# VectorE's program written out for all steps in a one-core attention and mixture-of-experts layer

## The reference

```
x = x + attention(layernorm(x))     # 16 heads, keys of 16, values of 64, no softmax: relu(q.k)^2
x = x + moe(layernorm(x))           # 16 experts of width 64, 4 chosen per token, plus a shared expert
```

## Time and profile before

| | us |
|---|---|
| median of three runs | 830.85 |
| lowest, highest | 829.86, 833.11 |
| the profiled execution, its own time | 831.47 |
| its span, first to last instruction | 829.5 |

### The profile page before, as it was taken

How to read it: one execution, slowest core, us unless ns; L and a number is a source line. 1 busy time by engine, 2 the same in 40 slices (tenths; PEclk the granted TensorE clock), 3 DMA queues, 4 the chain that set the end, 5 groups by cost and what they waited for, 6 DMA issues and landing times.

```text
span 829.5 us, 16902 instructions
## 1 busy us (share of the span) xinstructions
PE 691.8 (83%) x5160; PEld 545.1 (66%) x5160; DVE 520.7 (63%) x1739; ACT 434.9 (52%) x986; POOL 352.7 (43%) x368
## 2 busy tenths in 40 slices
PE   1576897979979797988979797997979799797785
PEld 1444476858767685867758585876758587676675
DVE  3545667576666748576575757667475856666654
ACT  2466674565646464564646456464655556453211
POOL 2246563644435353544535264453526444363100
PEclk9878998999989898998989899898989999898898
DMA  8994849091835619092562909174371908300000
GB/s 194 132 144 48 131 87 108 14 144 24 124 48 95 72 60 113 6 139 32 94 72 73 98 18 137 24 113 58 79 87 36 128 1 126 40 15 1 8 7 7
DMA packets 72814, 60.94 MB, mean 73 GB/s; under 512 B 8624, under 2 KB 72496, under 8 KB 72752
## 3 DMA queue, kind: packets, MB, share of 16 engines
q1 hardware_dynamic: 72752, 60.26, 49.4%
HBM read 41.37 MB, written 18.87 MB: 73 GB/s over the span
## 4 chain that ended last, share of the span: by engine, by line
PE 57%; DVE 25%; issue 9%; ACT 4%; DMA 2%; DVEq 1%; POOL 1%; SPq 1%; ACTq 0%; POOLq 0%
PE ps_a L503 11%; PE ps_f L365 8%; PE ps_f L428 7%; PE ps_f L367 6%; PE ps_f L366 6%; PE ps_f L447 5%; PE ps_s L474 5%; PE ps_f L424 4%; DVE norms_m L741 2%; PE ps_f L407 2%; DMA qkt<-qk_rows 2%; DVE it L852 2%; PE ps_f L418 2%; DVE norms_t L661 2%; DVE norms_t L662 2%
## 5 line engine op out<-in xcount | busy, mean ns | idle before, releaser
L334 POOL TENSOR_TENSOR p<-r 128x512 f32<-128x512 f32 x256 | 262.5, 1046 | 392.4 <-ACT r L603 392.4
L603 ACT ACTIVATE r<-ps_s 128x512 f32<-128x512 f32 x256 | 138.5, 596 | 81.0 <-PE ps_s L474 79.8
L503 PE MATMUL ps_a<-p,v 128*64 128x256 f32 x1024 | 143.5, 396 | 3.4 <-DVE big L897 2.2
L897 DVE TENSOR_TENSOR big<-ps_a,wt 128x256 f32<-128x256 f32 x128 | 53.7, 420 | 73.7 <-ACT big L612 51.1
L503 PEld LDWEIGHTS ps_a<-p,v 128*64 128x64 f32 x1024 | 64.4, 138 | 41.7 <-POOL p L334 2.7
L852 DVE TENSOR_TENSOR it<-ps_f,it 128x256 f32<-128x256 f32 x144 | 59.1, 420 | 44.0 <-ACT it L595 41.0
L595 ACT ACTIVATE it<-ps_f 128x256 f32<-128x256 f32 x144 | 55.2, 383 | 50.1 <-PE ps_f L367 47.7
L418 PE MATMUL ps_f<-ident,cs 128*32 128x128 f32 x32 | 9.2, 387 | 83.8 <-DVE cs L787 83.8
L447 PE MATMUL ps_f<-wdown,it 128*128 128x128 f32 x576 | 71.2, 279 | 2.9 <-DVE it L869 1.7
L869 DVE TENSOR_TENSOR it<-ps_f,it 128x512 f32<-128x512 f32 x64 | 44.0, 690 | 44.8 <-PE ps_f L424 44.3
L447 PEld LDWEIGHTS ps_f<-wdown,it 128*128 128x128 f32 x576 | 68.4, 195 | 4.5 <-DVE it L869 1.8
(11 more groups left out here) (153 smaller groups left out, 1607.2 us busy)
## 6 DMA issues: line engine op xcount, KB each, us to landing
qk_rows<-qk_parts SPq DMA_DIRECT2D x16, 1024.0 KB, 4.4
qkt<-qk_rows SPq DMA_DIRECT2D x64, 256.0 KB, 9.5
qkt<-qk_rows SPq DMA_DIRECT2D x128, 128.0 KB, 8.9
x_in<-in_L_attn_tokens SPq DMA_DIRECT2D x16, 128.0 KB, 2.2
x_res<-in_L_attn_tokens SPq DMA_DIRECT2D x16, 128.0 KB, 14.4
out<-o_sb SPq DMA_DIRECT2D x16, 128.0 KB, 14.2
big<-in_L_attn_Wqg SPq DMA_DIRECT2D x1, 640.0 KB, 4.2
big<-in_L_attn_Wkv SPq DMA_DIRECT2D x1, 640.0 KB, 5.3
```

The source lines that it names most:

```text
L334: pool.tensor_tensor(p[h % 4][:], r[h % 2][:], r[h % 2][:], ALU.mult).then_inc(probs_done, 1)
L503: last = pe.matmul(ps_a[k % 2][64 * e:64 * e + 64, 0:N], v[q][:, t, h * DV:(h + 1) * DV], p[h % 4][:, t * N:(t + 1) * N], start=(t == 0), ...
L603: act.activation(r[h % 2][:], ps_s[h % 2][:], ACT.Relu).then_inc(relu_done, 1)
L897: dve.tensor_tensor(aw[ap][:, pair, :], ps_a[pair % 2][:, 0:N], wt[ap][:, pair, :], ALU.mult)\
```

## The change

A second walker, `run_flat`, writes all 20 steps out, and VectorE uses it in place of `run_steps`. The steps of VectorE hold the same instructions on the same data in the same order. Every wait gets a constant, and the register instructions and the branch of the loop are gone from VectorE's program. For steps 4 to 13 the program text now has ten copies of a step where it had two. Nothing changes for the other four engines; TensorE, ScalarE and GpSimd keep the loop with register values.

```
+        def run_flat(step):
+
+            for s in range(FIRST_STEP, LAST_STEP + 1):
                 step(s, s % 2, stages(s), s)
...
-            run_steps(dve, step)
+            run_flat(step)
```

More of the change, by code:

```diff
@@ L200, in run_steps @@
             for s in range(LOOP_TO, LAST_STEP + 1):
+                step(s, s % 2, stages(s), s)
+        def run_flat(step):
+            for s in range(FIRST_STEP, LAST_STEP + 1):
                 step(s, s % 2, stages(s), s)
```

## The result

| | before | after |
|---|---|---|
| median, us (lowest, highest) | 831.24 (829.86, 833.11) | 820.25 (819.13, 821.27) |
| the profiled execution | 831.47 | 821.27 |
| its span | 829.5 | 819.5 |
| ratio to before, 95% interval | | 0.9863 [0.9847, 0.9879] |

The change makes the kernel faster by 1.4%, 11.0 us by the medians and 10.2 us between the two profiled executions. Lines behind the added function stand five further down: 787, 418 and 836 are now 792, 423 and 841.

What follows compares the result with a forecast made beforehand. The chain through TensorE and VectorE's small instructions ahead of `cs` was taken to bound the kernel. Jumps 4.1, registers 2.9 and 0.2 sum to 7.2 us, raised to 8.0 for the clock: 830.85 to 822.9, range 817 to 829.5.

Steps and rivals of the forecast that it cites:

- (3): TensorE's clock behind each restart: faster steps fall out of step with its rises; total gain taken as 8.0 us, not 7.2.
- What bounds the kernel: Chain through TensorE, VectorE's small dependent instructions and back with `cs`; VectorE's losses ahead of line 787 move TensorE's restart.
- fixed parts: Interval between TensorE restarts less 0.42 times the low-clock time: 44.99 written out, 45.28 in the loop, 46.30 with a jump.
- (1): VectorE's four jumps back go: each stalls 4.3 us, 1.02 us of it reaching the restart; 4.1 us, bounds 0 to 17.3.
- (2): VectorE's register work in steps 4 to 13 goes: 0.29 us a step, 2.9 us, plus 0.2 for the interval into step 4.
- Sum at an unchanged clock: Savings from VectorE's jumps and register work, with the low clock unchanged: 4.1 + 2.9 + 0.2 = 7.2 us.
- low stretches: Time TensorE runs at 1.2 GHz behind each restart, 2.71 to 5.78 us; each microsecond loses 0.42 us.
- the walk's first case: Stepping restarts against clock rises 47.8 us apart: one rise comes 3.4 us sooner in the 5.9 us step; 9.4 us gained.
- the second case: The early clock rise comes one step after the 5.9 us stretch; average stays 4.4 us and the gain is 7.2.
- Rival (a): Steps stay in step with clock rises if the fixed part exceeds 45.36 us, eating the gain: 829 to 833 us; chance 0.14.
- (c): TensorE, ScalarE or GpSimd needs its own reload at its loop's jump, returning 4.1 us: 827.0 us; chance 0.05.
- (d): VectorE's longer written-out program stalls while loading, 4.3 us a time: slower, 835 us or more; chance 0.05.

Runs made afterwards that it cites:

- the hint: The kernel before with its loop kept on VectorE and a branch hint at the head of each round: 828.13 us, ratio 0.9963.
- The pair of runs with 15 matmuls: 15 overwritten 128x512 matmuls per step ahead of TensorE's wait for `cs`: kernel before 801.98 us, changed kernel 793.04 us.
- the changed kernel with 36 matmuls: Changed kernel plus 36 overwritten 128x256 matmuls per step ahead of TensorE's wait for `cs`: 858.19 us, one of four executions 802.48.
- The stand-in at slot 0: Changed kernel plus 16 small dependent VectorE instructions at the head of slot 0 in steps 6, 8, 10 and 12: 835.35 us, ratio 1.0067.

## Why the prediction was right, and where it was off

Forecast 822.9 in 817.0 to 829.5; measured 820.25. The direction and the mechanism were right; the gain was 11.0 us where I had 8.0, and the shape of the steps came out right for a reason that is in part luck (see (3)).

- **What bounds the kernel: right.** The restarts behind the wait for `cs` move with everything VectorE loses ahead of line 787 and with the clock. Intervals without the low clock fall to the fixed parts within 0.2 us.
- **(1) The jumps: right in kind and in size.** Without jumps but with registers the fixed part is 45.26 where it was 46.30 and 45.28. Instructions to be loaded were the cause, since the hint removes the stall. The Trainium skill (Runtime: NRT & Kernel Launch, Instruction fetch mechanics) says that an engine loads its program ahead in sequence, so that a long program need not fit, and that a taken jump to a part no longer held must wait for it. The trace agrees: the longest wait of the kind "issue" in VectorE's 20 written-out steps is 0.3 us.
- **(2) The register work: this is the term that was mis-sized.** I had 0.29 us a step, 45.28 - 44.99, and bounds of 0 and 3.1 for the ten steps. It is 45.26 - 44.80 = 0.46, 4.6 us and 4.8 with the outlier, outside the bounds; the restart wait itself goes from 5.32 to 4.87 us. The reference 44.99 came from steps in which GpSimd was written out too. I had asked whether the other engines' constants made it too good; they made it too bad by 0.19 us, some 0.13 of it from GpSimd, whose instructions with its loop happen to lie better against VectorE's. Over ten steps this is 1.9 us.
- **Sum at an unchanged clock.** The fixed parts average 45.71 before and 44.80 after the earlier trace rows, 9.1 us in ten steps and not 7.2. The pair of runs with 15 matmuls gives 8.9 once the three low stretches are taken off.
- **(3) The clock: right in kind.** The low stretches of 2.7, 4.6, 5.6 and back to 2.8 look like the walk's first case, but the forecast's own fixed part of 44.99 would not have given them: all engines written out, at 44.98, gave the second case, with 5.9 us reached and ten intervals 7.2 us shorter than before. The walk had the early rise start from a low stretch of 5.9 us; the runs show stretches up to 6.01. The short one came in every third step because the fixed part was 0.19 us below the forecast. The average went from 4.38 to 4.22, worth 0.7 us, about the 0.8 that I had put on top of 7.2. The first case was also summed too high: walked again with the same numbers it gives 9.2 us, not 9.4.
- **Rival (a), the beat.** It did not happen here, but the run with registers and no jumps is close to it: with a fixed part of 45.26 most of the gain is taken back. The point at which the steps stay with the rises was put too high: with stretches up to 6.0 us it is 47.8 - 0.42 x 6.0 = 45.28, not 45.36. So the forecast's margin was 0.29 us and not 0.37, and the measured one is 0.48.
- **Rivals (c) and (d).** Neither showed. (c) is real for TensorE once its round grows by 144 instructions, and not with 60. The length of the round tells the engines of the kernel before apart: between two of its branches the trace holds 391 instructions of VectorE, which reloads, and 233 of ScalarE and 105 of GpSimd, which do not. TensorE does not with 1435 and 1493 and does with 1577.

What stays open: why one execution of the changed kernel with 36 matmuls had no stalls of TensorE while three had, and how GpSimd's register work changes the stretching of VectorE's instructions by 0.03 to 0.06 us each. The stand-in at slot 0 doesn't give the cover of the jump's stall more closely than the intervals did.

## What to carry to other kernels

In this kernel the jump back of a loop cost VectorE, with 391 instructions a round, a reload of 4.3 us each time, while engines with shorter rounds had none. Where a trace shows such a wait of the kind "issue" behind a branch, write the program out or give the loop a branch hint, and look at the chain to see how much of it shows. Where a step contains one long wait of TensorE, read the granted clock behind it before adding up: savings can be taken back by a longer low stretch (4.1 us gave 2 to 3), and a further small saving can release them (0.46 us a step gave 8.4). Work that fills such a wait and ends ahead of its release was then worth more than either, 27 to 29 us here, as long as it doesn't make that engine's own loop reload.

## What the runs showed of the hardware that was not expected

- The same instruction of VectorE, 128x64 on one tile, took 0.214 us at the least, 0.226 at the median and 1.108 at the most in the run with the stand-in at slot 0. In each of the four places 4 of the 16 took 0.96 to 1.11 us, and these lie beside GpSimd's pairs of instructions, which take 2.04 us each. Sixteen of them took 7.31 us there and 5.10 in slot 2.
- The clock's rise is tied to more than the time since the restart: behind waits of 4.87 to 5.83 us the low stretch was 2.6 to 6.0 us, behind four waits of 9.00 us it was 3.9 to 5.5.
- TensorE's program reloads at its jump with 144 more matmuls and weight loads in a round, 9 to 12 us each time in two pieces, and not at all with 60 more.
